# First attention on Trainium2: narrow scores in one product, and two transposed heads in one bank

## The reference, cut to what matters

```python
# attention A on the standardised x: 16 heads of 16 columns, scale 1/4, stride 22
scores = einsum('bhqd,bhkd->bhqk', q, k) * scale
strided = causal & ((i - j < stride) | (j % stride == i % stride))                # heads 0 to 7
fixed = causal & ((j // stride == i // stride) | (j % stride >= stride - 1))      # heads 8 to 15
attn = softmax(where(mask, scores, min)); out = (attn @ v) @ Wo.T
# the weights of the feed-forward block, in blocks of 16
scale = max(abs(w)) / 6; wq = nearest(w / scale) * sign * scale
```

## Time and profile before

| What | Value |
|---|---|
| median of 3 runs | 3564.15 us (3558.09 to 3564.78) |
| profiled execution, its own time | 3559.97 us |
| its span, first to last instruction | 3558.2 us |
| mean granted TensorE clock | 0.944 |
| TensorE matmul, busy | 3088.3 us, 87% |
| VectorE, busy | 2790.0 us, 78% |
| ScalarE, busy | 2184.9 us, 61% |
| GpSimd, busy | 1121.6 us, 32% |
| attention A | from 1.8 to 1060 us of the span |
| weight preparation | from 1060 to 1132 us |

### The profile page before, as it was taken

The page is one execution under the profiler, slowest core; times in us unless marked ns, Lnnn a source line. Parts: engine busy times, 40 slices in busy tenths (PEclk is TensorE's granted clock), DMA queues, the critical chain, the costliest instruction groups (busy, mean ns, idle before and its releaser), DMA issues. The chain is left out here.

```text
span 3558.2 us, 70567 instructions
## 1 busy us (share of the span) xinstructions
PE 3088.3 (87%) x24024; PEld 2396.3 (67%) x24024; DVE 2790.0 (78%) x7209; ACT 2184.9 (61%) x5360; POOL 1121.6 (32%) x664
## 2 busy tenths in 40 slices
PE   6999999999985999995888888888888886799998
PEld 4666666666664888884556556656655654688888
DVE  4776777767767999993778888888888887699997
ACT  3777777777762343432777877777777775344443
POOL 1000000000004555553123444433333333455554
PEclk9999999999996999997898989989999997899999
DMA  4344443434422000001344444334434433111000
GB/s 90 46 70 62 62 71 45 70 62 63 63 37 102 13 19 19 19 19 30 48 61 69 62 72 72 60 60 67 72 60 67 71 54 89 42 36 32 29 30 24
DMA packets 134182, 190.46 MB, mean 54 GB/s; under 512 B 15126, under 2 KB 81558, under 8 KB 133142
## 3 DMA queue, kind: packets, MB, share of 16 engines
q1 hardware_dynamic: 133830, 185.95, 30.3%
HBM read 45.65 MB, written 28.84 MB: 21 GB/s over the span
## 5 line engine op out<-in xcount | busy, mean ns | idle before, releaser
L409 ACT ACTIVATE a_probs<-a_probs,a_negmax 128x176 f32<-128x176 f32 (+4 forms) x1024 | 502.6, 491 | 265.7 <-DVE a_negmax L330 259.8
L330 DVE CUSTOM_DVE_ANT_0 a_probs<-a_mask,a_score 128x176 f32<-128x176 f32 (+4 forms) x1024 | 404.1, 401 | 270.5 <-PE a_score L486 114.4
L1718 DVE CUSTOM_DVE_ANT_0 b_u<-b_u,b_score 128x512 f32<-128x512 f32 x512 | 340.8, 682 | 135.3 <-PE b_score L1973 132.8
L494 PE MATMUL a_turned<-ident,a_probs 128*128 128x128 f32 (+1 forms) x2176 | 411.4, 280 | 37.7 <-DVE a_pT L339 29.7
L1843 ACT ACTIVATE b_u<-b_u,b_negmax 128x512 f32<-128x512 f32 x512 | 367.1, 717 | 112.0 <-DVE b_negmax L1718 110.4
L1247 PE MATMUL f_y_bank<-f_wdT,f_hqT 128*128 128x256 f32 x1536 | 357.0, 382 | 40.6 <-ACT f_hqT L1186 36.9
L1710 DVE SCALAR_TENSOR_TENSOR b_u<-b_u,b_score 128x1024 f32<-128x1024 f32 x256 | 310.0, 1215 | 93.5 <-ACT b_u L1836 91.1
L1836 ACT ACTIVATE b_u<-b_score 128x1024 f32<-128x1024 f32 x256 | 262.0, 1024 | 162.3 <-PE b_score L1963 161.9
L1247 PEld LDWEIGHTS f_y_bank<-f_wdT,f_hqT 128*128 128x128 f32 x1536 | 284.6, 190 | 89.5 <-issue 56.4
L1982 PE MATMUL b_turned<-ident,b_u 128*128 128x128 f32 x2048 | 320.6, 281 | 24.9 <-DVE b_pT L1724 19.5
L1982 PEld LDWEIGHTS b_turned<-ident,b_u 128*128 128x128 f32 x2048 | 248.6, 145 | 97.1 <-issue 59.9
(11 more groups left out here) (236 smaller groups left out, 7132.1 us busy)
## 6 DMA issues: line engine op xcount, KB each, us to landing
b_stack<-b_part SPq DMA_DIRECT2D x192, 256.0 KB, 8.2
a_stack_q<-a_part SPq DMA_DIRECT2D x192, 128.0 KB, 4.3
a_stack_k<-a_part SPq DMA_DIRECT2D x192, 128.0 KB, 5.3
xs<-in_x_dram SPq DMA_DIRECT2D x16, 512.0 KB, 8.5
x_before_b<-xs SPq DMA_DIRECT2D x16, 512.0 KB, 2.9
b_xin<-x_before_b SPq DMA_DIRECT2D x16, 512.0 KB, 12.2
b_xres<-x_before_b SPq DMA_DIRECT2D x16, 512.0 KB, 3.9
x_after_b<-b_xres SPq DMA_DIRECT2D x16, 512.0 KB, 5.8
```

The lines of the kernel that those rows point to most:

```text
L330: dve.tensor_tensor_reduce(out=probs[:, n % 2, j, 0:keys(n)], in0=mask_of(n), in1=score[j][:, 0:keys(n)], scale=-1.0, scalar=3.0e38, op0=A ...
L409: act.activation(probs[:, n % 2, j, 0:keys(n)], probs[:, n % 2, j, 0:keys(n)], ACT.Exp, bias=negmax[:, n, j:j + 1], scale=-1.0, accum_out= ...
L494: m = nc.tensor.transpose(turned[j % 2][0:rows, u, :], chunk(n, probs[:, n % 2, j, :], u), ident[:])
L1718: dve.tensor_tensor_reduce(out=u[:, n, j, :], in0=u[:, n, j, :], in1=score[:, j, :], scale=-0.05, scalar=3.0e38, op0=ALU.add, op1=ALU.min, ...
```

## The change

In attention A, K1 (the keys of the second half of the heads) is written to its part in three pieces, for the whole first tile, the far keys three times over, and the near keys of three tiles: 128 + 3 * 176 = 656 columns. The new stack wide_k takes them, and the narrow scores become one product of 176 columns. Groups of at most two chunks (n = 0 to 3 and 8 to 15) turn heads 0 and 1 side by side into turned[0] and heads 2 and 3 into turned[1]; VectorE copies the first pair with one instruction after its masking of head 1, ScalarE the second with one after its exponential of head 3.

In weight preparation the seven loads that fold_heads needs have a semaphore of their own, and the work is in another order: the x front goes behind the weights on GpSimd, VectorE and ScalarE, the turns of w_down ahead of fold_down on TensorE.

```diff
+A_WIDE = P + (TILES - 1) * A_NARROW
...
-        part = sb("part", [P, 2, 2, SEQ], FP32R)
+        part = sb("part", [P, 2, 2, A_WIDE], FP32R)
         stack_q = sb("stack_q", [P, 2, 2, 4, SEQ], FP32R)
-        stack_k = sb("stack_k", [P, 2, 4, SEQ], FP32R)
+        stack_k = sb("stack_k", [P, 4, SEQ], FP32R)
+        wide_k = sb("wide_k", [P, 4, A_WIDE], FP32R)
...
+        def paired(n):
+            return chunks(n) <= 2
...
+        def part_pieces(job, row):
+            if job != "K1":
+                return [row[:, 0:SEQ]]
+            blocks = row[:, P:A_WIDE].rearrange("p (t w) -> p t w", w=A_NARROW)
+            return [row[:, 0:P], blocks[:, :, 0:A_FAR], blocks[:, :, A_FAR:A_NARROW]]
...
+        def side_pieces(job):
+            if job != "K1":
+                return [side[:]]
+            far = side[:, A_STRIDE - 1:A_STRIDE * A_FAR:A_STRIDE].unsqueeze(1).to_broadcast([P, TILES - 1, A_FAR])
+            return [side[:, 0:P], far, near_columns()]
...
+        def near_columns():
+            near = side[:, P - A_NEAR:2 * P]
+            return bass.AP(near.tensor, near.offset, [list(near.ap[0]), [P, TILES - 1], [1, P + A_NEAR]])
...
                 for b, h in enumerate(((0, 0, 1), (0, 1, 0))[i]):
                     for e in range(2):
-                        frm = part[64 * e:64 * e + 64, i, h, :].bitcast(FP32)
+                        frm = part[64 * e:64 * e + 64, i, h, 0:(A_WIDE if job == "K1" else SEQ)].bitcast(FP32)
                         at = slice(64 * e + 16 * b, 64 * e + 16 * b + 16)
-                        to = stack_k[at, c, :, :] if i else stack_q[at, e, c, :, :]
+                        to = (wide_k if c else stack_k)[at, :, :] if i else stack_q[at, e, c, :, :]
                         sp.dma_start(to.bitcast(FP32), frm).then_inc(s_placed[c], 16)
...
-            sp.wait_ge(s_zero, 4)
+            sp.wait_ge(s_zero, 5)
...
             pool.memset(stack_k[:].bitcast(FP32), 0.0).then_inc(s_zero, 1)
+            pool.memset(wide_k[:].bitcast(FP32), 0.0).then_inc(s_zero, 1)
             pool.memset(v_rest[:], 0.0).then_inc(s_zero, 1)
...
                 if job[0] in "QK":
                     i = "QK".index(job[0])
                     dve.wait_ge(s_hi, parts_before(s, job) + 1)
-                    dve.scalar_tensor_tensor(out=part[:, i, 1, :], in0=side[:], scalar=(0.25, 1.0)[i],
-                                             in1=part[:, i, 0, :], op0=ALU.mult, op1=ALU.subtract).then_inc(s_free, 1)
+                    for low, high, src in zip(part_pieces(job, part[:, i, 1, :]), part_pieces(job, part[:, i, 0, :]),
+                                              side_pieces(job)):
+                        m = dve.scalar_tensor_tensor(out=low, in0=src, scalar=(0.25, 1.0)[i], in1=high,
+                                                     op0=ALU.mult, op1=ALU.subtract)
+                    m.then_inc(s_free, 1)
...
                 t = chunks(n)
-                dve.tensor_copy(pT[:, n % 2, j, 0:t, :], turned[0][:, 0:t, :]).then_inc(s_mv_v, 1)
+                if paired(n):
+                    both = turned[0][:, 0:2 * t, :].rearrange("p (j t) q -> p j t q", j=2)
+                    dve.tensor_copy(pT[:, n % 2, 0:2, 0:t, :], both).then_inc(s_mv_v, 2)
+                else:
+                    dve.tensor_copy(pT[:, n % 2, j, 0:t, :], turned[0][:, 0:t, :]).then_inc(s_mv_v, 1)
...
                     for j in range(4):
                         if kind != "tail":
                             mask_max(s, n, j)
-                        if j in (0, 2) and turned_group:
+                        if turned_group and j in ((1,) if paired(turned_group[1]) else (0, 2)):
                             move_turned(*turned_group, j)
...
-                    act.activation(part[:, i, 0, :], side[:], ACT.Copy, scale=(0.25, 1.0)[i]).then_inc(s_hi, 1)
+                    for high, src in zip(part_pieces(job, part[:, i, 0, :]), side_pieces(job)):
+                        m = act.activation(high, src, ACT.Copy, scale=(0.25, 1.0)[i])
+                    m.then_inc(s_hi, 1)
...
-                act.activation(pT[:, n % 2, j, 0:t, :], turned[1][:, 0:t, :], ACT.Copy).then_inc(s_mv_a, 1)
+                if paired(n):
+                    both = turned[1][:, 0:2 * t, :].rearrange("p (j t) q -> p j t q", j=2)
+                    act.activation(pT[:, n % 2, 2:4, 0:t, :], both, ACT.Copy).then_inc(s_mv_a, 2)
+                else:
+                    act.activation(pT[:, n % 2, j, 0:t, :], turned[1][:, 0:t, :], ACT.Copy).then_inc(s_mv_a, 1)
...
                     for j in range(4):
                         if kind != "tail":
                             exps(s, n, j)
-                        if j in (0, 2) and turned_group:
+                        if turned_group and paired(turned_group[1]):
+                            if j == 3:
+                                move_turned(*turned_group, 3)
+                        elif turned_group and j in (0, 2):
                             move_turned(*turned_group, j + 1)
...
                 if narrow(n):
-                    far = slice(A_STRIDE - 1, A_STRIDE * A_FAR, A_STRIDE)
-                    mm(score[j][:, 0:A_FAR], q, stack_k[0:112, c, j, far], start=True, stop=True)
-                    m = mm(score[j][:, A_FAR:A_NARROW], q, stack_k[0:112, c, j, t * P - A_NEAR:(t + 1) * P],
+                    at = P + (t - 1) * A_NARROW
+                    m = mm(score[j][:, 0:A_NARROW], q, wide_k[0:112, j, at:at + A_NARROW], start=True, stop=True)
+                else:
+                    m = mm(score[j][:, 0:keys(n)], q, (wide_k if c else stack_k)[0:112, j, 0:keys(n)],
                            start=True, stop=True)
-                else:
-                    m = mm(score[j][:, 0:keys(n)], q, stack_k[0:112, c, j, 0:keys(n)], start=True, stop=True)
                 m.then_inc(s_score, 1)
...
             def turn_head(s, n, j):
                 pe.wait_ge(s_prob, s * 64 + 4 * n + j + 1)
-                wait(pe, (s_mv_v, s_mv_a)[j % 2], s * 32 + 2 * n + j // 2)
+                b, before = (j // 2, 0) if paired(n) else (j % 2, j // 2)
+                first = j % 2 * chunks(n) if paired(n) else 0
+                wait(pe, (s_mv_v, s_mv_a)[b], s * 32 + 2 * n + before)
                 for u in range(chunks(n)):
                     rows = A_REST if narrow(n) and u else P
-                    m = nc.tensor.transpose(turned[j % 2][0:rows, u, :], chunk(n, probs[:, n % 2, j, :], u), ident[:])
+                    m = nc.tensor.transpose(turned[b][0:rows, first + u, :], chunk(n, probs[:, n % 2, j, :], u), ident[:])
                 m.then_inc(s_turn, 1)
...
+        s_heads = sem("head_weights_loaded")
...
-        loads = [(wqT, "b_wqT"), (wkT, "b_wkT"), (c2q, "b_c2q"), (bq, "b_bq"), (bk, "b_bk"), (bv, "b_bv"), (bc, "b_bc"),
-                 (w1T, "b_w1T"), (wm, "b_wm"), (b1, "b_b1"), (bm, "b_bm"), (wqoT, "b_wqoT"), (bqo, "b_bqo"),
-                 (w2, "b_w2"), (wq_in, "b_wq"), (bq_in, "b_bq_turned"), (w["bk"], "b_bk_turned"), (w["wk"], "b_wk"),
-                 (w["wv"], "b_wv"), (w["wo"], "b_wo"), (w["rows"], "b_rows"), (w["sum8"], "b_sum8")]
+        head_loads = [(wqT, "b_wqT"), (wkT, "b_wkT"), (c2q, "b_c2q"), (bq, "b_bq"), (bk, "b_bk"), (bv, "b_bv"),
+                      (w["wo"], "b_wo")]
+        loads = [(w1T, "b_w1T"), (wm, "b_wm"), (b1, "b_b1"), (wqoT, "b_wqoT"), (bqo, "b_bqo"), (w2, "b_w2"),
+                 (bc, "b_bc"), (bm, "b_bm"), (wq_in, "b_wq"), (bq_in, "b_bq_turned"), (w["bk"], "b_bk_turned"),
+                 (w["wk"], "b_wk"), (w["wv"], "b_wv"), (w["rows"], "b_rows"), (w["sum8"], "b_sum8")]
...
+            for dst, name in head_loads:
+                sp.dma_start(dst[:], a[name]).then_inc(s_heads, 16)
             for dst, name in loads:
...
             front.pool_norm(pool, 0)
             divide(0)
             divide(1)
-            front.pool_divide(pool, 0)
             scale(0)
             pool.wait_ge(s_deq, 2)
             divide(2)
             scale(1)
+            scale(2)
+            front.pool_divide(pool, 0)
             front.pool_scale(pool, 0)
-            scale(2)
...
             front.vector_norm(dve, 0)
             scales(0)
             scales(1)
-            front.vector_scales(dve, 0)
             mark(0)
             scales(2)
             mark(1)
-            front.vector_round(dve, 0)
             for n in range(4):
                 move(n)
             mark(2)
+            front.vector_scales(dve, 0)
+            for n in range(4, 8):
+                move(n)
             dve.wait_ge(s_deq, 1)
-            for n in range(4, len(turns)):
+            for n in range(8, len(turns)):
                 move(n)
+            front.vector_round(dve, 0)
+            dve.wait_ge(s_heads, 16 * len(head_loads))
             dve.wait_ge(s_w, 16 * len(loads))
...
             front.scalar_standard(act, 0)
             magnitude(0)
+            magnitude(1)
+            for n in range(4):
+                high(n)
```

(14 more changed lines are left out.)

## The result

The changed kernel takes 3627.35 us (median of 4 runs, 3620.52 to 3635.36) against 3563.18 for the kernel before (4 runs, 3558.09 to 3564.78): a ratio of 1.0187, 95% interval 1.0168 to 1.0207. The profiled execution has a span of 3622.0 us, 63.8 more than before. Attention A ends at 1129.2 instead of 1059.3 (+69.9), and weight preparation takes 67.2 us from there to its last instruction instead of 73.1 (-5.9).

What follows compares the result with a forecast made beforehand. Attention was taken as bound by a ring of waits among TensorE, VectorE and ScalarE. Attention +33, start +0.8 and preparation -6.4 gave +27.4 us, 3587 for the profiled execution and 3592 for the median; range 3540 to 3612.

Steps and rivals of the forecast that it cites:

- The walk: Attention, slot by slot: timed each masking, exponential and copy from the start of a weighting; total +2.2 us a sequence.
- K1's pieces: Slot 14: three pieces, 656 columns, instead of one cost +0.22 us on ScalarE and +0.30 on VectorE.
- the narrow product: Narrow scores in attention: one product fewer gains at most 0.43 us a slot; -0.4 each in slots 11 and 13.
- +2.2 a sequence; 15 sequences place K and Q for the next, so +33 us: Attention: the slot terms summed to +2.2 us a sequence, over 15 sequences +33 us.
- in slot 12 it misses that by 1.5 us: Slot 12: ScalarE's copy ends 1.5 us too late to hide behind TensorE's two heads of the next slot.
- upper bound, +54: Attention: if all twelve paired slots lost 0.3 us besides, +54 us.
- Preparation: Weight preparation after attention: the new order gains 6.4 us, with ends of 3.1 and 9.
- The start: Start of the kernel: larger zeroing of K's stacks and K1's low part before the first masking, +0.8 us once.
- The transfers: K1's six DMA transfers, 656 columns instead of 512, issued in slot 14 and needed in slot 8: 0 us.
- The sign by which it was to be known: Profile after: weightings 3.5, 3.7 and 4.2 us apart, TensorE's wait before them ended by ScalarE's copy; a 65.5 us sequence.
- TensorE is the bound: Rival, chance 0.15: in attention the late copy hides behind TensorE's work in all slots; about 3510 to 3530 us.
- The ring gives way in part: Rival, chance 0.27: following covered slots take back the lateness of slots 12 and 4; 3550 to 3570 us.

Runs made afterwards that it cites:

- e2_pair: Kernel before with only the pairs of heads (two narrow products, K1 in one part, old preparation): 3619.03 us, ratio 1.0168.
- e5_fill: Changed kernel plus 24 products adding zero in front of the weighting in slots 11, 13 and 15: 3609.79 us, ratio 1.0140 against the kernel before.
- e1_narrow: Kernel before with only the wide key rows and single narrow product, no pairs, old preparation: 3558.71 us, ratio 0.9994.
- e6_pair_early: Kernel before with the pairs alone, ScalarE's copy behind the exponential of head 2: 3562.56 us, ratio 1.0007.
- e8_late_only: Kernel before with only ScalarE's copy of head 3 moved behind the exponential of head 3, no pairs or wide keys: 3705.39 us, ratio 1.0402.
- e4_early: Changed kernel with ScalarE's pair copy after the exponential of head 2 instead of head 3: 3544.82 us, ratio 0.9958 against the kernel before.

## Why the prediction came out as it did

The direction was right, and so was the mechanism as far as the working had it: the late copy makes the weighting wait. The time lies above the range: +64 us against a forecast of +27. Most of the missing 36 us is a price that the working did not have.

**The walk.** It put the parts of slot 12, from the start of the weighting, at 1.7 (low part), 2.3 (fourth masking), 2.65 (its exponential), 3.1 (the copy) and 3.7 (its end). They came at 1.70, 2.30, 2.67, 3.12 and 3.70, and the next weighting at 3.83. The table has it term by term. A slot is here the distance from its weighting to the next slot's, from weight load to weight load (0.03 off the rows of the products in places); the values are medians over the sequences 1 to 14, without slots at half clock, in us a sequence. The forecast's -0.24 for the first two heads of slot 10 stands in the row of slot 9, since those heads come before slot 10's weighting:

| Slots | Forecast | Measured |
|---|---|---|
| 10 | +0.35 | 2.80 to 3.22, +0.42 |
| 11 | -0.4 | 3.94 to 3.53, -0.41 |
| 12 | +0.8 | 2.91 to 3.80, +0.89 |
| 13 | -0.4 | 4.17 to 3.75, -0.42 |
| 14 | +1.3 | 2.92 to 4.32, +1.40 |
| 15 and 0 | +0.3 | 5.50 to 6.06, +0.56 |
| 1 and 9 | -0.59 | 8.49 to 7.80, -0.69 |
| 2 to 5 | +0.85 | 16.69 to 17.98, +1.29 |
| all | +2.2 | +3.0 |

K1's pieces were priced at 0.22 and 0.30, at the low ends, and cost 0.24 and 0.28. Two terms were sized too small: slots 2 to 5 by 0.4, and slots 15 and 0 by 0.3; no run shows which wait makes up either difference. With the 0.1 of slots 10, 12 and 14 each, less the 0.1 of slots 1 and 9, this makes 0.8 a sequence, 12 us of the 36. In the changed kernel the narrow product gave what was forecast: against e2_pair, which lacks it, slots 11 and 13 are shorter by 0.4 each and slot 9 by 0.2.

**The step that failed** is the sum "+2.2 a sequence; 15 sequences place K and Q for the next, so +33 us": it has no term for TensorE's clock, and took all durations of TensorE at the clock of the rows before, 1.00. The walk itself had put a standstill of 1.5 us in front of a weighting ("in slot 12 it misses that by 1.5 us"), and asked only who waits then, not what it does to TensorE's clock. The rows it started from gave no warning: that clock was 1.00 in attention, with waits of up to 1.1 us. What the runs showed: half-clock stretches, 17 in the sequences 1 to 14, cost 1.45 us a sequence there, 20 us in all (e5_fill). The working knew the lower clock, 0.54 in weight preparation, and used it there alone. Its upper bound, +54, has the same gap, and a slip of its own: it is 15 x 12 x 0.3 alone, without the +33 that it is said to come "besides". Together they are +87, and the time measured would have been inside that bound, for a wrong reason. Most of the 4 us left lies in the first sequence (65.16 us against 59.65, with three stretches at half clock instead of one) and in the last.

**The other steps.** Preparation was forecast at -6.4 and gave -5.9; the products of the folding ended 65.5 us after attention (forecast 65.0). The new order did not only remove a collision of VectorE and GpSimd and "add none": with the x scales gone from ahead of it, the first marking runs beside a division and takes 5.55 instead of 2.22. So mark(0) ends 25.3 us after attention where the walk had 24.4, and mark(1) 36.8 where it had 36.1, about the 0.5 by which the stage missed its forecast. The start cost +1.0, forecast +0.8. The transfers cost nothing, as said. The sign by which it was to be known, TensorE's wait "ended by ScalarE's copy", holds in the timelines, while the view of waits names VectorE. The weightings stand apart as it said: 3.80 us in slot 12 (3.7), 4.32 in slot 14 (4.2), 3.53 in slot 11 (3.5). A sequence takes 66.17 us without half clock, not 65.5.

**The rivals.** "TensorE is the bound" does not hold. In the changed kernel the late copy is not hidden, as the 67.9 us of waits show, and in e1_narrow, without it, the 24 products taken away are worth 0.7 us a sequence, not 2.6, and K1's pieces take 0.5 of it back. "The ring gives way in part" was wrong too: the covered slots 11 and 13 gave 0.4 each, as in the walk, and took nothing back. The Trainium skill says that breaking instructions up may let work be completed sooner where ScalarE and VectorE aren't saturated but cause bubbles elsewhere (Perfetto Trace Analysis, Optimizing Scalar/DVE Operations). That pointed the right way, but the runs narrow it down: the grouped copies by themselves, in the early place, changed the time by nothing that can be told (1.0007, e6_pair_early), and 2% hung on what stood ahead of them.

## What to carry to other kernels

When copies are merged, ask first at which place of the consumer's order the merged one ends; put it where its inputs are ready and nothing slower stands ahead, here ahead of the last exponential, not behind it. Where a change makes TensorE wait longer or more often in a stage that it fills (here from at most 1.1 us to 1.4 to 2.5 us), add the price of its work at half clock behind the wait as an upper end, and look in the profile at the granted clock and at whether equal repetitions take equal time. The best kernel here, pairs in the second half of the heads with the early copy, wide key rows and the new preparation, takes 3536 us against 3560 in the same comparison.

## What the hardware showed unexpectedly

TensorE's clock fell to its lower level inside a stage in which TensorE is busy 54 of 66 us. In the changed kernel it fell behind standstills of 1.4 to 2.5 us, while the same standstills in other sequences left it at 1.00. In e8_late_only it also fell where no wait of the 8 us before was over 0.4 us, and in e4_early it stayed up through waits of 1.5 us, so no length of a single wait tells these runs apart. It came and went from one sequence to the next with the same instructions, and giving TensorE more work made the kernel about 17 us faster. The Trainium skill's page TensorE: Matmul & The Clock Gate, section A second HAM failure mode: psum-queue depth-cycling, tells of a kernel whose short idle times between groups of products make the clock go down and up. This trace agrees, with 17 stretches in 949 us.
